# Second attention of a five-sublayer kernel: exponentials kept in fp32 for the value products

## What is computed

```python
q, k, v = x @ Wq, x @ Wk, x @ Wv          # 16 query heads, 4 key/value heads of 8 features
k, v = (repeat of each key/value head for 4 query heads)
q, k = _rope(q, cos, sin), _rope(k, cosk, sink)
scores = einsum('bhqd,bhkd->bhqk', q, k) / sqrt(128)
p = softmax(scores)                        # over 256 keys, no mask
o = einsum('bhqk,bhkd->bhqd', p, v)
return o.reshape(B, S, D) @ Wo
```

## Time and profile before

| | |
|---|---|
| median of three runs | 1822.4 us |
| the profiled execution, first to last instruction | 2151.2 us |
| second attention in it, from the first `scores` to the last addition | about 1219.7 to 1595.5 us |
| busy over the whole span | PE 60%, DVE 53%, POOL 45%, ACT 36% |
| granted TensorE clock, mean | 0.730 of 2.4 GHz |

### The profile page before, as it was taken

How to read it: one execution, slowest core, us unless ns; L and a number is a source line. 1 busy time by engine, 2 the same in 40 slices (tenths; PEclk the granted TensorE clock), 3 DMA queues, 4 the chain that set the end, 5 groups by cost and what they waited for, 6 DMA issues and landing times.

```text
span 2151.2 us, 34449 instructions
## 1 busy us (share of the span) xinstructions
PE 1289.1 (60%) x11544; PEld 930.5 (43%) x11545; DVE 1132.4 (53%) x2864; ACT 781.4 (36%) x1164; POOL 970.1 (45%) x1052
## 2 busy tenths in 40 slices
PE   2496578736921424987743387777750513997762
PEld 1495466526820113976511144444430201986621
DVE  6445677672478101423533699889978200333442
ACT  1243366613410001533211188888850100443310
POOL 0623155523225764034462267667633766024464
PEclk9997799957955766999775555555555755998885
DMA  7232144102200112444310000000000111444321
GB/s 303 82 88 73 57 159 152 57 12 86 76 25 31 48 67 67 149 137 123 92 48 22 11 2 2 3 2 2 2 1 20 48 66 52 137 141 129 108 74 49
DMA packets 100126, 150.60 MB, mean 70 GB/s; under 512 B 21520, under 2 KB 54928, under 8 KB 99216
## 3 DMA queue, kind: packets, MB, share of 16 engines
q1 hardware_dynamic: 58768, 75.30, 11.0%
q0 software_dynamic: 20480, 41.98, 6.7%
q10 hardware_dynamic: 20736, 31.47, 4.3%
HBM read 74.16 MB, written 74.45 MB: 69 GB/s over the span
## 4 chain that ended last, share of the span: by engine, by line
PE 33%; DVE 19%; another core or an unknown queue 17%; issue 15%; ACT 4%; POOL 4%; SPq 4%; DMA 3%; ACTq 1%; DVEq 0%; POOLq 0%
PE PS L910 6%; PE PS L932 3%; PE PS L847 3%; SPq L1349 2%; PE PS L300 2%; PE PS L302 2%; PE PS L301 2%; PE PS L1793 2%; PE PS L918 2%; POOL AREA L1100 2%; POOL slots_top L626 2%; DVE AREA L1959 2%; DVE X L1123 1%; DVE XN L409 1%
## 5 line engine op out<-in xcount | busy, mean ns | idle before, releaser
L1100 POOL DMA_INDIRECT AREA<-results_top,ROW x320 | 305.3, 954 | 516.5 <-DMA results_top<-AREA 330.1
L626 POOL DMA_INDIRECT slots_top<-XN,ROW x320 | 318.2, 995 | 319.0 <-DVE ROW L580 185.8
L742 DVE SCALAR_TENSOR_TENSOR AREA<-PS,AREA 128x512 f32<-128x512 f32 x64 | 43.8, 691 | 323.2 <-issue 181.2
L910 PE MATMUL PS<-WGU,AREA 128*128 x768 | 192.7, 396 | 13.7 <-ACT AREA L974 13.7
L1754 POOL TENSOR_TENSOR AREA<-AREA 128x1024 f16<-128x1024 f32 x64 | 151.4, 2365 | 91.6 <-ACT AREA L1894 91.4
L1011 DVE SCALAR_TENSOR_TENSOR AREA<-PS,AREA 128x512 f32<-128x512 f32 x96 | 66.4, 692 | 218.0 <-ACT AREA L985 170.9
L712 ACT ACTIVATE AREA<-PS 128x512 f32<-128x512 f32 x64 | 38.1, 598 | 373.7 <-remote 293.9
L1983 DVE TENSOR_REDUCE AREA<-PS 128x4 f32<-128x1024 f32 x128 | 156.1, 1219 | 25.4 <-PE PS L1781 24.7
L1887 ACT ACTIVATE AREA<-PS,AREA 128x1024 f32<-128x1024 f32 x128 | 142.7, 1115 | 53.5 <-PE PS L1793 53.5
L910 PEld LDWEIGHTS PS<-WGU,AREA 128*128 128x128 f32 x768 | 146.3, 201 | 32.9 <-ACT AREA L974 15.0
L932 PE MATMUL PS<-WD,AREA 128*128 x768 | 112.5, 293 | 53.3 <-DVE AREA L1006 46.2
(11 more groups left out here) (261 smaller groups left out, 3636.4 us busy)
## 6 DMA issues: line engine op xcount, KB each, us to landing
AREA<-slots_top SPq DMA_DIRECT2D x96, 256.0 KB
results_top<-AREA ACTq DMA_DIRECT2D x96, 256.0 KB
slots_top<-ZERO SPq DMA_DIRECT2D x24, 512.0 KB, 3.1
AREA<-slots_top SPq DMA_DIRECT2D x48, 128.0 KB
results_top<-AREA ACTq DMA_DIRECT2D x48, 128.0 KB
AREA<-query_rows SPq DMA_DIRECT2D x48, 128.0 KB, 2.9
slots_top<-XN,ROW POOLq DMA_INDIRECT x320
AREA<-results_top,ROW POOLq DMA_INDIRECT x320
```

Source lines behind the costliest of these rows:

```text
L626: nc.gpsimd.indirect_dma_start(out=L.xs[q], out_offset=bass.IndirectOffsetOnAxis(ap=ROW[:, n:n + 1], axis=0), in_=XN[:, t * D:(t + 1) * D] ...
L910: ins = nc.tensor.matmul(o, XTF[:, v, j * P:(j + 1) * P], w, start=True, stop=True)
L1100: nc.gpsimd.indirect_dma_start(out=slots[L.tag][u][:, c * D:(c + 1) * D], out_offset=None, in_=L.ys[g * GT // L.tiles], in_offset=bass.Ind ...
```

## The change

Only `attn1` is changed, and the order of rows in the laid-out Wo.

- The exponentials stay in fp32. PF1 becomes two buffers, one for even and one for odd tiles; `phi` on ACT and `plo` on DVE and POOL are removed, with PB1.
- `values(c-1, n)` runs for n = 0 in round 1, 1 in round 2, 2 and 3 in round 3. n stands for (odd heads or not, key tile k). Each has four matmuls, one for each head group g: stationary V32 of tile k and group g, 128x32 fp32 (eight value columns, a one, and zeros: a band of its own for each group), moving 256 columns of fp32 exponentials, output in partitions 32g to 32g+32 of bank 6. So the sums come out with features on the partitions and queries on the columns.
- ACT copies the whole bank 6 (512 columns) to OS in round 0; PE turns it back with four fp32 transposes into bank 7 in round 1 (`values_turned`); DVE's `norm` reads bank 7 directly, in round 2.
- The normed output ON is transposed once in fp32, one turn later, in round 0, into free columns of bank 0; ACT copies it to OT; the output product is one fp32 matmul with AOF (Wo in fp32), in round 1, also into bank 0; DVE adds it to x in round 1, `statistics` moves to round 3 ahead of `rope`. The projection of tile c+5, in the same bank, also waits for that addition.
- The split of Wo and of the values is removed. V32 holds eight tiles and is zeroed on POOL at the start.
- One more turn is written out at the end.

```diff
-        PF1 = area([4, 1024], F32)
-        PB1 = [area([4, 1024], F16) for _ in range(2)]
-        OS = area([16 * 17], F32)
+        PF1 = [area([4, 1024], F32) for _ in range(2)]
+        OS = area([4 * P], F32)
...
-            ones = VP[:, :, :].rearrange("p t (g c) -> p t g c", c=17)[:, :, :, 8]
-            nc.gpsimd.memset(ones, 1.0).then_inc(b_cst.sem, 1)
+            nc.gpsimd.memset(V32, 0.0).then_inc(b_cst.sem, 1)
...
-            def values(i, c, g):
+            def values(i, c, n):
+
                 t = i * 8 + c
-                wait_split(pe, i, c, g)
-                if g == 0:
-                    wait(pe, b_oc, t)
-                for r in range(4):
-                    o = (4 * g + r) * 17
-                    for k in range(2):
-                        v = VP[:, bass.ds(i * 8 + c // 2 * 2 + k, 1), g * 17:(g + 1) * 17].rearrange("p a c -> p (a c)")
-                        at = (r % 2 * 4 + k * 2 + r // 2) * P
-                        p = [PB1[n][:, g, at:at + P] for n in range(2)]
-                        nc.tensor.matmul(banks(6)[:, o:o + 17], p[0], v, start=k == 0, stop=False)
-                        ins = nc.tensor.matmul(banks(6)[:, o:o + 9], p[1], v[:, 0:9], start=False, stop=k == 1)
+                odd, k = divmod(n, 2)
+                wait(pe, b_exp, 4 * t + 4)
+                wait(pe, b_oc, t)
+                for g in range(4):
+                    at = odd * 512 + k * 256
+                    ins = nc.tensor.matmul(banks(6)[32 * g:32 * (g + 1), odd * 256:(odd + 1) * 256],
+                                           V32[:, (c // 2 * 2 + k) % 8, g, :], PF1[c % 2][:, g, at:at + 256],
+                                           start=k == 0, stop=k == 1)
                 ins.then_inc(b_pv.sem, 1)
+
+            def values_turned(i, c):
+
+                t = i * 8 + c
+                wait(pe, b_oc, t + 1)
+                wait(pe, b_on, t)
+                for odd in range(2):
+                    for half in range(2):
+                        at, r = (odd * 2 + half) * P, 2 * half + odd
+                        ins = nc.tensor.transpose(banks(7)[:, r * P:(r + 1) * P], OS[:, at:at + P], IDF[:, :])
+                ins.then_inc(b_vt.sem, 1)
...
-                wait(pe, b_vlo, t)
+                wait(pe, b_rope, t)
+                wait(pe, b_oadd, t - 7)
...
-                    before = c - 1 if g < 3 else c
-                    if tile_exists(i, before):
-                        values(i, before, (g - 3) % 4)
+                    if g > 0 and tile_exists(i, c - 1):
+                        values(i, c - 1, g - 1)
+                    if g == 3 and tile_exists(i, c - 1):
+                        values(i, c - 1, 3)
...
-                    if g == 1 and tile_exists(i, c - 2):
-                        wait(pe, b_olo, t - 1)
-                        wait(pe, b_oadd, t - 2)
-                        for n in range(2):
-                            ins = nc.tensor.transpose(banks(7).bitcast(F16)[:, n * P:(n + 1) * P], ONB[n][:, :],
-                                                      IDH[:, :])
-                        ins.then_inc(b_otr.sem, 1)
+                    if g == 0 and tile_exists(i, c - 3):
+                        wait(pe, b_on, t - 2)
+                        wait(pe, b_rope, t + 5 if tile_exists(i, c + 4) else NT)
+                        if not tile_exists(i, c + 4):
+                            wait(pe, b_oadd, t - 3)
+                        nc.tensor.transpose(banks(0)[:, 352:480], ON[:, :, :].rearrange("p h c -> p (h c)"),
+                                            IDF[:, :]).then_inc(b_otr.sem, 1)
...
+                    if g == 1 and tile_exists(i, c - 2):
+                        values_turned(i, c - 2)
+                    if g == 1 and tile_exists(i, c - 3):
+                        wait(pe, b_ot, t - 2)
+                        nc.tensor.matmul(banks(0)[:, 352:480], OT, AOF, start=True, stop=True).then_inc(b_y.sem, 1)
...
-                    if g == 3 and tile_exists(i, c - 2):
-                        wait(pe, b_ot, t - 1)
-                        product3(banks(7)[:, 0:D], [OTB[:, n * P:(n + 1) * P] for n in range(2)],
-                                 [AO[n][:, :] for n in range(2)]).then_inc(b_y.sem, 1)
...
-                if tile_exists(i, c - 1):
-                    wait_split(act, i, c - 1, g)
-                nc.scalar.activation(PF1[:, g, :], banks(4, 2), ACT.Exp, bias=LNSP[:, 0:1],
+                if tile_exists(i, c - 2):
+                    wait(act, b_pv, 4 * (i * 8 + c) - 4)
+                nc.scalar.activation(PF1[c % 2][:, g, :], banks(4, 2), ACT.Exp, bias=LNSP[:, 0:1],
                                      scale=SCALE1).then_inc(b_exp.sem, 1)
 
-            def phi(i, c, g):
-                n = 4 * (i * 8 + c) + g
-                wait(act, b_exp, n + 1)
-                wait(act, b_pv, n - 3)
-                nc.scalar.activation(PB1[0][:, g, :], PF1[:, g, :], ACT.Copy).then_inc(b_phi.sem, 1)
+            def values_copy(i, c):
+                t = i * 8 + c
+                wait(act, b_pv, 4 * t + 4)
+                wait(act, b_vt, t)
+                nc.scalar.activation(OS, banks(6), ACT.Copy).then_inc(b_oc.sem, 1)
...
                     if g == 0 and tile_exists(i, c - 2):
-                        wait(act, b_on, t - 1)
+                        values_copy(i, c - 2)
+                    if g == 0 and tile_exists(i, c - 3):
                         wait(act, b_otr, t - 2)
-                        nc.scalar.activation(ONB[0][:, :], ON[:, :, :].rearrange("p h c -> p (h c)"), ACT.Copy
-                                             ).then_inc(b_ohi.sem, 1)
+                        nc.scalar.activation(OT, banks(0)[:, 352:480], ACT.Copy).then_inc(b_ot.sem, 1)
...
-                wait(dve, b_oc, t + 1)
-                os = OS[:, :].rearrange("p (h c) -> p h c", c=17)
-                nc.vector.tensor_tensor(ON[:, :, :], os[:, :, 0:8], os[:, :, 9:17], ALU.add)
-                nc.vector.reciprocal(RC[:, :], os[:, :, 8]).then_inc(b_nstep.sem, 1)
+                wait(dve, b_vt, t + 1)
+                wait(dve, b_otr, t)
+                o = banks(7).rearrange("p (n c) -> p n c", c=32)
+                nc.vector.reciprocal(RC[:, :], o[:, :, 8]).then_inc(b_nstep.sem, 1)
```

More of the change, by code:

```diff
@@ L223, in build @@
         AW = [area([352], F16, 0), area([352], F16)]
-        AO = [area([D], F16) for _ in range(2)]
+        AOF = area([D], F32)
         COS, SIN = (area([2, 160], F32) for _ in range(2))
@@ L231, in build @@
         KT = area([4, 2, 2 * P], F16)
[L232 removed]
+        V32 = area([8, 4, 32], F32)
         QT1, QT2 = (area([2, 512], F16) for _ in range(2))
         MX = area([2, 16], F32)
[L235 to L237 removed]
+        PF1 = [area([4, 1024], F32) for _ in range(2)]
+        OS = area([4 * P], F32)
         ON = area([16, 8], F32)
         RC = area([16], F32)
[L240 to L242 removed]
+        OT = area([P], F32)
+        WST = PF1[0][:, 0, 0:352]
         STG = area([3, 2048], F32, 7680)
```

124 lines of the change are left out of this document (38 added, 86 removed).

## The result

The changed kernel takes 1746.1 us (median of 4 runs, 1744.5 to 1749.6) against 1822.3 (4 runs, 1816.0 to 1823.6): ratio 0.959, 95% interval 0.957 to 0.961. That is 76 us less, where 27 were forecast; the time lies outside the range.

The account below looks back on a forecast made before the run. Bound: PE's order of work plus two waits a turn in the second attention. Turns 0.81 us shorter give 20 us; fill and end 4, tail 2, weight split 0.4: 27 off 1822.4, 1795 us, range 1778 to 1854.

Parts of the forecast that it names:

- the value group: PE, four fp32 value matmuls on separate strips: run together, 0.45 us a group, 1.8 us a turn.
- My case: Second attention: turn 10.29 us against 11.10, kernel 1795 us, bounds 1779 to 1815, chance 0.60.
- rival A: Value groups cost double, by pairs only or twice the cycles: 55 us more, 1850 us, chance 0.12.
- rival C: Second attention's clock rises to 2.4 GHz, turn 7.9 us: about -85 us, 1737 us, chance 0.10.
- The two waits named as bounding: PE waits for L1959 in round 1 and L1915 in round 3: 1.05 and 1.21 us a turn, to go.
- rival B: The four matmuls of a value group run one after another: 164 us more, 1959 us, chance 0.09.
- The change of form: PE, between matmul forms: 0.13 us each, one more in rounds 1 and 2, +0.26 us a turn.
- The new wait in round 0: PE ready for `q_four` at 0.97 us, b_m from DVE at 1.53; round 0 takes 2.30 us.
- rival D: A wait replaces the removed ones: `rope` and bank-0 waits push round 0 to 3.1 us; 1816 us, chance 0.09.
- the two stops of 5.9 us: PE in the 24 steady turns before: two unexplained stops, one loop body of eight turns apart, 5.9 us in all.
- no round was to get under 1.99 us: Loop of exp and `by_key` through banks 4 and 5 closes in 1.99 us, a floor for every round.
- the tail: From last exp to last `statistics`: 8.0 us after against 10.0 before, 2 us less.

Follow-up runs that it names:

- the run with a wait per turn: Changed kernel plus one more TensorE wait at each turn's head, for VectorE's last rotary sum of the turn before; 2185.6 us, kernel before 2213.7 on the same chip.
- structure without the work: Changed kernel with exponentials and banded values in fp16 instead of fp32, one pass per value matmul; 2121.4 us, kernel before 2166.7 on the same chip.
- work without the structure: Kernel before plus one fp32 matmul per value group, 2314.8 us against 2166.7; with more: three per group, 2363.3; six per turn inside its pauses, 1832.2.
- the full-width run: Changed kernel with all four value strips as one 128-column stationary operand, value sums left wrong; 2218.3 us, kernel before 2166.7 on the same chip.

## Why the prediction was wrong

**The first wrong term: the value group.** "An fp32 column costs two fp16 columns" was read from transposes. A transpose of fp32 is one record, an fp32 matmul two, and each record costs two fp16 passes. At the old clock a group is 0.86 us and not 0.45, the output product 0.43 and not 0.21: 1.64 + 0.22 = 1.86 us a turn missing from the sum. Rounds that run wholly at 0.50 bear this out: round 2 took 3.40 (1054.39 to 1057.79 in turn 1), with the right price 2.94 + 0.41 = 3.35; in the run with a wait per turn rounds 1 took 3.5 to 3.6, with the right price 3.05 + 0.41 + 0.22 = 3.68, and one round 3 took 2.83, 2.00 + 0.82 = 2.82. My case with this put right is a turn of 10.29 + 1.86, about 12 us, against 11.10, a kernel some 30 us slower than before. So the mechanism of rival A was right and its place in the chances too low.

By that the trace agrees with the Trainium skill (FP8 and Floating Point Precision, TensorE Precision Notes), whose four passes I had set against the row of the transposes: 0.86 us for 256 columns at 1.2 GHz, where one pass takes 0.213. That section speaks of fp32 products; of transposes, which took two here, it says nothing.

**The second wrong term: the clock.** Every PE price was taken at 0.50. That stretches of the stage would be granted 2.4 GHz was rival C, at 0.10, 1737 us with turns of 7.9; measured were 1746 and warm turns of 8.22. (C's own terms, 32 x 3.2 less 10, give 92 us and not 85, so 1730.) What I had against it was that "the new turn stops and changes form as often". It stops for 1.05 us a turn, where before did for 2.3. And TensorE had more to do per turn than I knew, by the first wrong term. The runs show both to count: structure without the work 0.58, work without the structure 0.51 or, with more of it, 0.85 to 0.87, both 0.92 to 0.94. The two errors go in opposite directions, so it is not from the first that the kernel came out faster than forecast, but from the second; and the second hangs on the first: with one-pass values the clock stays low.

The Trainium skill (TensorE: Matmul & The Clock Gate, Part 1) calls the lower level the default, which activity releases. The runs with fillers agree: idle TensorE time filled with useless matmuls made the stage 14 us shorter.

**What was right.** The two waits named as bounding are gone (no wait on ScalarE in round 3, none on VectorE in round 1), and with VectorE's work put back 63 of the 74 to 76 us are lost again, half of them by the clock. How much of the gain is the waits alone is not shown. The strips run side by side: rival B is refuted, by 7 ns between starts and by the full-width run. The change of form is 0.13 to 0.16 us at 0.50. The new wait in round 0, for the maxima ahead of `q_four`, is there: 0.4 us, forecast 0.56; rival D, which made it 1.4, is out. **What else was off:** the two stops of 5.9 us were left in the sum and are gone; no round was to get under 1.99 us, and with one-pass values rounds 3 take 1.91 at 0.50, in the changed kernel warm rounds 1.69 and 1.82; the tail takes 1.1 us more, not 2 less; the fp32 groups and turned sums in it run at 0.50 again.

**How the 76 us stand, then.** New structure at nearly the old clock with one-pass values: 50 (350.3 to 300.3), of which 6 are the two stops. The clock's rise, less the cost of four passes instead of one: another 24 to 26. Cost of the passes and gain of the clock can't be told apart further: no run held the changed kernel at 0.50. What it would take there, some 12 us a turn, is worked out and not shown as a whole turn.

## What to carry to other kernels

Price an fp32 matmul from an fp32 matmul of the same kind in the trace, never from a transpose: count records per instruction first. Before multiplying PE durations by a clock, ask whether the change removes the pauses of a stage that runs at half clock, and make the sum at both levels; but look whether another engine's order sets the turn, since then the second level gives nothing. Where turns of a stage fall back from the upper level, a useless matmul inside a wait that is there anyway is worth trying: here 14 us of the stage for two added lines.

## What the runs showed of the hardware

- An fp32 matmul stands in the trace as two MATMUL records and two weight loads (903 and 896 for 448 matmuls of L1789 in the window above), each record as long as two fp16 passes; an fp32 transpose is one record.
- Four matmuls on four strips of 32 output partitions start 6 to 7 ns apart and take the time of one.
- A filler of one fp32 matmul of 128 columns a turn lifted the granted clock of the stage from 0.92 to 1.00. The longest wait of TensorE was 0.8 us with and without it.
- The other chips take about 340 to 390 us longer for the same kernel; for the changed kernel, profiled on both, none of it is in the second attention. Waits of the changed kernel, first on a chip where it takes 1745 us, then on one where it takes 2139 (there the wait of L710 is put down to "remote"; on the first chip L710 waits 133.9 us for PE):

```profile
POOL AREA L1098 <- DMA results_top<-AREA: 90.8, 6, 28.2
```

```profile
POOL AREA L1098 <- DMA results_top<-AREA: 361.3, 8, 104.6
ACT AREA L710 <- remote: 342.5, 25, 31.7
```

The expert stages wait there for transfers of results and for something outside the core. What it is stays open.
